# Channel-major partitions for the tiles of the first cross-attention of a gated two-layer block

## What is computed

```
x = x + tanh(g_xattn[0]) * L0_xattn(ctx, ctx, layernorm(x), ssm_kernel, D)
x = x + tanh(g_ffn[0])   * L0_ffn(layernorm(x), w1, b1, w2, b2)
x = x + tanh(g_xattn[1]) * L1_xattn(layernorm(x), ctx, ...)
x = x + tanh(g_ffn[1])   * L1_ffn(layernorm(x), ...)

L0_xattn: 32 heads of 8 channels; for channels i, j of one head
  kv[b,i,j,h,l] = ctx[b,i,h,l] * ctx[b,j,h,l]
  y = causal convolution of kv over l with ssm_kernel[h], plus D[h] * kv
  out[b,j,h,l] = sum over i of y[b,i,j,h,l] * q[b,i,h,l]
L0_ffn: int8 quantised linear 512 -> 2048, gelu, int8 quantised linear 2048 -> 512
```

## Time and profile before

| | |
|---|---|
| median of three runs | 734.99 us |
| the profiled execution's own time | 737.37 us |
| its span | 735.6 us |
| PE busy | 629.7 us (86%) |
| DVE busy | 547.1 us (74%) |
| ACT busy | 487.4 us (66%) |
| POOL busy | 345.8 us (47%) |
| bytes moved by DMA | 118.91 MB |

### The profile page before, as it was taken

How to read it: one execution, slowest core, us unless ns; L and a number is a source line. 1 busy time by engine, 2 the same in 40 slices (tenths; PEclk the granted TensorE clock), 3 DMA queues, 4 the chain that set the end, 5 groups by cost and what they waited for, 6 DMA issues and landing times.

```text
span 735.6 us, 9513 instructions
## 1 busy us (share of the span) xinstructions
PE 629.7 (86%) x2838; PEld 370.0 (50%) x2838; DVE 547.1 (74%) x1068; ACT 487.4 (66%) x726; POOL 345.8 (47%) x435
## 2 busy tenths in 40 slices
PE   3618619889999897992999999999989799999997
PEld 3416417667777663441454445555554344444443
DVE  2120636786899788781977799998998899999975
ACT  1302126757769656781997733776776999999985
POOL 1121445776878561750200001110336888989862
PEclk7667769999999998896999999999999999999999
DMA  3323466669999994123149199200012366656561
GB/s 107 116 105 119 140 198 222 221 206 318 343 282 330 403 300 160 54 103 138 57 126 357 44 171 249 66 14 14 15 29 57 116 172 173 190 169 198 155 188 43
DMA packets 127861, 118.91 MB, mean 162 GB/s; under 512 B 83456, under 2 KB 90384, under 8 KB 126672
## 3 DMA queue, kind: packets, MB, share of 16 engines
q1 hardware_dynamic: 120120, 103.71, 46.1%
q10 hardware_dynamic: 7704, 14.76, 6.3%
HBM read 68.04 MB, written 30.49 MB: 134 GB/s over the span
## 4 chain that ended last, share of the span: by engine, by line
PE 52%; DVE 14%; ACT 9%; SPq 8%; DMA 7%; issue 6%; POOL 2%; ACTq 0%; DVEq 0%; POOLq 0%
PE ps L1240 15%; PE ps L1502 12%; PE ps L1518 7%; PE ps L1330 4%; SPq L382 4%; ACT turn L1020 4%; PE ps L1429 3%; PE ps L1459 3%; SPq L391 2%; DMA arena<-in_x 2%; DMA x_d<-arena 2%; SPq L475 2%; PE ps L1477 2%; PE ps L1433 1%; DMA tern_d<-late 1%
## 5 line engine op out<-in xcount | busy, mean ns | idle before, releaser
L1240 PE MATMUL ps<-arena 128*128 128x288 f32 x640 | 174.7, 431 | 33.5 <-ACT arena L789 17.5
L1240 PEld LDWEIGHTS ps<-arena 128*128 128x128 f32 x640 | 127.0, 203 | 71.2 <-issue 20.2
L1502 PE MATMUL ps<-arena 128*128 128x512 bf16 x512 | 113.7, 379 | 4.3 <-DVE arena L2094 4.3
L629 POOL TENSOR_TENSOR arena<-arena 128x1024 f32<-128x1024 f32 x31 | 58.7, 1894 | 60.7 <-PE ps L1251 34.2
L733 POOL TENSOR_TENSOR arena<-arena 128x512 f32<-128x512 f32 x64 | 80.4, 1279 | 8.9 <-DVE arena L2094 8.1
L1502 PEld LDWEIGHTS ps<-arena 128*128 128x128 bf16 x512 | 49.6, 98 | 66.3 <-DVE arena L2094 3.6
L1330 PE MATMUL ps<-arena 128*128 128x512 bf16 (+1 forms) x256 | 61.2, 399 | 15.0 <-ACT arena L970 13.9
L1653 DVE TENSOR_TENSOR turn<-ps,arena 128x768 f32<-128x768 f32 x32 | 30.6, 955 | 43.4 <-PE ps L1251 43.3
L970 ACT ACTIVATE arena<-ps,b,s 128x512 f32<-128x512 f32 x64 | 46.1, 787 | 23.2 <-DMA x_d<-arena 15.3
L1518 PE MATMUL ps<-arena 128*128 128x512 bf16 x256 | 58.2, 379 | 1.0 <-ACT arena L1134 0.7
L1371 PE MATMUL ps<-arena 128*128 128x512 bf16 x256 | 55.6, 379 | 0.4 <-DVE arena L1843 0.4
(11 more groups left out here) (225 smaller groups left out, 1310.4 us busy)
## 6 DMA issues: line engine op xcount, KB each, us to landing
arena<-in_L_ffn_w SPq DMA_DIRECT2D x48, 512.0 KB, 6.4
arena<-kpad_d ACTq DMA_DIRECT2D x16, 512.0 KB, 6.0
hq_d<-arena SPq DMA_DIRECT2D x14, 512.0 KB, 2.6
tern_d<-late SPq DMA_DIRECT2D x24, 256.0 KB, 6.0
arena<-in_x SPq DMA_DIRECT2D x16, 256.0 KB
arena<-in_L_ffn_w ACTq DMA_DIRECT2D x8, 512.0 KB, 4.7
arena<-in_ctx SPq DMA_DIRECT2D x2, 2048.0 KB
x_d<-arena SPq DMA_DIRECT2D x16, 256.0 KB
```

The source lines that it names most:

```text
L629: pool.tensor_tensor(dst[:, :, 0:32].rearrange("p r (d i) -> p r d i", d=4), a, shifted, ALU.mult)
L1240: last = pe.matmul(ps[:, 4 * s + lo, 0:NB * PAIRS], toep[:, u, (LB - 1 - lo + li) * P:(LB - lo + li) * P], kv[:, s, li, :], start=(li == 0 ...
L1502: last = pe.matmul(ps[:, bank, :], xq4T[:, s, 4 * j + k, :], w[:, k, c * L:(c + 1) * L], start=(k == 0), stop=(k == LB - 1))
```

## The change

The partitions of a tile now hold 4 * channel + batch. All that touches this order follows:

- Loads and the stores to `x1_d` name 32 channels outermost and four batches inside, where they named four batches and then 32 channels. Bytes, the length of one contiguous piece (2 KB), number and order of the DMAs stay the same.
- `ctxT` and `qT` hold batch innermost. The eight channels of a head are then 16 bytes apart for each batch, so that `head_rows` yields single values 16 bytes apart instead of runs of eight. `repeat_c`, `repeat_q` and the last addition of a head go through it.
- `repeat_q` is written as two instructions of 256 values instead of one of 512, because of the number of dimensions.
- `rows_out` copies straight, without reordering. The rows of the quantised layer are thus in the order tile, channel, batch up to Gelu, whose output pattern restores batch, tile, channel: consecutive values are written 512 bytes apart.

```diff
-        ctxT = cut(32, ROWS * DM).rearrange("p (g r c) -> p g r c", g=2 * G, r=ROWS)
+        ctxT = cut(32, ROWS * DM).rearrange("p (g a c b) -> p g a c b", g=2 * G, a=2 * LB, b=G)
...
         def head_rows(m, h):
-            return m[:, h // G, :, HD * (h % G):HD * (h % G) + HD]
+            return m[:, h // G, :, HD * (h % G):HD * (h % G) + HD, :].rearrange("p a c b -> p a b c")
+
+        def by_batch(m):
+            return m.rearrange("p (a b) i -> p a b i", b=G)
...
-            return rows.rearrange("(s b) (g c) l -> s g b c l", b=G, c=CG)[n % 2, n // 2]
+            return rows.rearrange("(s b) (g c) l -> s g c b l", b=G, c=CG)[n % 2, n // 2]
...
-                        sp.dma_start(x1_d[at:at + CG, first:first + 2 * G - 1:2, :].rearrange("c b l -> b c l"),
+                        sp.dma_start(x1_d[at:at + CG, first:first + 2 * G - 1:2, :],
                                      tile_home(x_res[:, order1[n], :])).then_inc(S["x1_saved"], 16)
...
-                pool.tensor_tensor(head_rows(qT, h), x[:, :, 0:8], x[:, :, 8:16], ALU.add).then_inc(S["o_done"], 1)
+                pool.tensor_tensor(head_rows(qT, h), by_batch(x[:, :, 0:8]), by_batch(x[:, :, 8:16]), ALU.add).then_inc(S["o_done"], 1)
...
-                act.activation(cdup[:, u, :, 0:8], csr, ACT.Copy)
-                act.activation(cdup[:, u, :, 8:12], csr[:, :, 0:4], ACT.Copy).then_inc(S["cd_ready"], 1)
+                act.activation(by_batch(cdup[:, u, :, 0:8]), csr, ACT.Copy)
+                act.activation(by_batch(cdup[:, u, :, 8:12]), csr[:, :, :, 0:4], ACT.Copy).then_inc(S["cd_ready"], 1)
...
-                act.activation(qdup[:, u].rearrange("p r (d i) -> p r d i", d=2),
-                               head_rows(qT, h).unsqueeze(2).to_broadcast([P, ROWS, 2, 8]),
-                               ACT.Copy).then_inc(S["qd_ready"], 1)
+                for first in (0, 8):
+                    last = act.activation(by_batch(qdup[:, u, :, first:first + 8]), head_rows(qT, h), ACT.Copy)
+                last.then_inc(S["qd_ready"], 1)
...
-                    act.activation(hid[:, q, f, :], ps[:, f % 4, :],
+                    act.activation(hid[:, q, f, :].rearrange("p (b j c) -> p j c b", b=G, j=G),
+                                   ps[:, f % 4, :].rearrange("p (j c b) -> p j c b", b=G, j=G),
                                    ACT.Gelu, bias=b1[:, f:f + 1], scale=s1[:, f:f + 1]).then_inc(S["gelu_done"], 1)
...
-                    src = bank_bf(4 + 2 * (g % 2), 2).rearrange("p (j k b c) -> p j k b c", j=G, k=LB, b=G)
-                    dst = xqT[:, :, g * L:(g + 1) * L].rearrange("p k (b j c) -> p j k b c", b=G, j=G)
-                    last = v.tensor_copy(dst[:, tiles], src[:, tiles])
+                    last = v.tensor_copy(xqT[:, :, g * L:(g + 1) * L].rearrange("p k (j n) -> p j k n", j=G)[:, tiles],
+                                         bank_bf(4 + 2 * (g % 2), 2).rearrange("p (j k n) -> p j k n", j=G, k=LB)[:, tiles])
```

More of the change, by code:

```diff
@@ L89, in flamingo_gated_block @@
         x_res = cut(0, NT * L).rearrange("p (t l) -> p t l", t=NT)
-        ctxT = cut(32, ROWS * DM).rearrange("p (g r c) -> p g r c", g=2 * G, r=ROWS)
+        ctxT = cut(32, ROWS * DM).rearrange("p (g a c b) -> p g a c b", g=2 * G, a=2 * LB, b=G)
         xn1 = [cut(at, NT // 2 * L).rearrange("p (b l) -> p b l", b=NB) for at in (112, 48)]
-        qT = cut(64, ROWS * DM).rearrange("p (g r c) -> p g r c", g=2 * G, r=ROWS)
+        qT = cut(64, ROWS * DM).rearrange("p (g a c b) -> p g a c b", g=2 * G, a=2 * LB, b=G)
         ctx_raw = [turn[:, n * L:(n + 1) * L] for n in range(8)] + [cut(112 + 2 * n, L) for n in range(8)]
@@ L349, in channels @@
         def channels(m, n):
-            return m[:, n // 2].rearrange("p (l h b) c -> p l h (b c)", l=LB, h=2)[:, :, n % 2, :]
+            return m[:, n // 2].rearrange("p (l h) c b -> p l h (c b)", h=2)[:, :, n % 2, :]
         def back_rows(n, l):
-            at = l * NB + n % 2 * G
-            return qT[:, n // 2, at:at + G, :].rearrange("p b c -> p (b c)")
+            return qT[:, n // 2, 2 * l + n % 2].rearrange("p c b -> p (c b)")
         def head_rows(m, h):
-            return m[:, h // G, :, HD * (h % G):HD * (h % G) + HD]
+            return m[:, h // G, :, HD * (h % G):HD * (h % G) + HD, :].rearrange("p a c b -> p a b c")
+        def by_batch(m):
+            return m.rearrange("p (a b) i -> p a b i", b=G)
         def backwards(row):
@@ L1718, in _ @@
             dv.wait()
-            v.tensor_tensor(head_rows(qT, HEADS - 1), x[:, :, 0:8], x[:, :, 8:16], ALU.add).then_inc(S["o_done"], 1)
+            v.tensor_tensor(head_rows(qT, HEADS - 1), by_batch(x[:, :, 0:8]), by_batch(x[:, :, 8:16]), ALU.add).then_inc(S["o_done"], 1)
             slot_add(TAIL - 1)
```

## The result

| | before | after |
|---|---|---|
| median | 735.27 us (4 runs, 734.73 to 737.88) | 692.27 us (4 runs, 690.51 to 693.5) |
| ratio | 1 | 0.9407, 95% interval 0.9376 to 0.9437 |
| profiled execution, own time | 737.37 us | 693.5 us |
| its span | 735.6 us | 691.7 us |
| PE busy | 629.7 us | 625.3 us |

The change saves 43 us. The forecast was 689 us, and its own range 680 to 700.

What follows compares the result with a forecast made beforehand. PE was taken to bound, ACT second, after an opening held up by four-engine tile loads. Terms -52 - 17 + 18 + 5 = -46 on 737.4 us gave 691, forecast 689 us as a median; range 662 to 704, own range 680 to 700.

Steps and rivals of the forecast that it cites:

- The opening: Tile loads before head 5: 16 DMA engines in place of four move head 5 from 109.3 to 57.3 us, -52 us.
- The stores: Stores to scratch in the quantised layer: ACT's 15.3 us wait goes and PE's 2.1 us of slower pace, -17 us.
- Gelu: Quantised layer: writes 512 bytes apart lengthen each Gelu from 0.79 to 1.2 us, 26 us of ACT, +18 come through.
- cover: ACT's idle ahead of its Gelus beyond the removed stores' wait, taken to hide 8 us of Gelu's 26 us excess.
- rival (A): ACT's writes and reads of values apart cost nothing; sum -68, 667 us; chance 0.30.
- The copies of a head: ACT's `repeat_c` and `repeat_q` in the heads: reads 16 bytes apart cost up to 0.7 us a head, +5 us.
- three late heads and three heads waiting for an x tile: Heads where ACT's slower copies were to show: late ones also widening weights, and those awaiting an x tile (0.7 us each).
- POOL's write: POOL's L638 in a head: at 2.8 ns a value already slower than a write of single values, 0 added.
- `rows_out`: DVE's copy keeps its length, as it already ran in long runs; 0.
- Rival (B): The opening gains a third less than 52 us, through HBM hops or Toeplitz loads meeting tiles; 706 us; chance 0.11.
- rival (C): DMAs still run on four engines, so the waits stay and only +18 and +5 remain; 758 us; chance 0.03.
- Rival (D): ACT pays several steps for each value apart, Gelu at 2.0 us; slower, about 775 us; chance 0.04.

Runs made afterwards that it cites:

- gelu_straight: The changed kernel, but Gelu writes adjacent values and the transposes of the quantised rows use an identity with permuted columns; 675.52 us, ratio 0.9153 to the kernel before.
- reads_adjacent: `gelu_straight` with `head_rows` naming eight adjacent values, so a head's batches and channels are mixed; 672.51 us, ratio 0.9098 to the kernel before.
- loads_25_7: The changed kernel with each tile load split into a DMA of 25 channels and one of 7; 723.08 us, ratio 0.9798 to the kernel before.
- gelu_ctx_straight: `gelu_straight` with context tiles also transposed against a permuted identity, so `repeat_c` reads runs of eight; 672.35 us, ratio 0.9107 to the kernel before.

## Why the prediction was right

**The opening, -52 us: -50.7.** The path was as laid out: `kpad` stored at 8.9 us (forecast 8.5), head 0 at 16.97 (15), head 1 at 29.43 (28.5), head 3 at 41.77 (41), head 5 at 58.59 (57.3). Most of the gap of 1.3 us arose before head 0: a context tile, issued behind the stop of SP, was waited for until 15.21 us. That the rate follows the outermost count is shown from both sides: 101 GB/s at four, 387 at thirty-two, 148 with 25 and 7, each with what else moved in its window. That agrees with the rule of the Trainium skill that the prediction cited (DMA: Bandwidth & Descriptors, section "Why a DMA increments its semaphore by 16 and not by 1"), by which these would be 4, 16, and 5 and 7 engines.

**The stores, -17 us: -15.4**, from `gelu_straight` against before. No instruction of ACT waits for the stores any more. The term was the sum of the wait (15.3) and 2.1 us of PE's slower pace; but since PE waits 13.5 us and not 15.3, 13.5 + 2.1 = 15.6 was the right sum: I counted the wait on ACT and the slowdown on PE.

**Gelu, +18 us: +16.7.** Forecast 1.2 us a Gelu, measured 1.34. The mean overstates it, since neighbours overlap: over the stage ACT is busy 21.2 us more, 0.33 us a Gelu, where I had 0.41 and 26. Of the 8 us that I took as cover only 4.5 were: ACT still idles 3.5 us ahead of its Gelus, 1.62 of it for PE's first result, as in `gelu_straight`. So the sum was 21.2 - 4.5, not 26 - 8, and that the term came out within 1.3 us is luck in part: an excess 5 us too large beside a cover 3.5 us too large. PE's own pace doesn't set the stage, since PE waits 13.2 us for Gelu in it. That this term exists at all was the choice against rival (A), which would have been 667; the pair L1655 and L1657 carried it, and its 0.8 ns a value stands beside 0.9 measured in the mean of single Gelus.

**The copies of a head, +5 us: +5.8, in part for other reasons.** Single copies cost what I took (L810 at 653 ns, forecast 0.6 us). But the reads account for only 2.2 us, in two heads. 1.4 us is a wait further on, 4.15 us in place of 2.73:

```profile
206.59 7.45 PE L1243 MATMUL ps<-arena 128*128 128x288 f32 x20 [4.15 <-POOL arena L632]
```

It stays in `reads_adjacent` (4.19 us), so taking the strides away doesn't remove it. In all these kernels ACT waits for a weight DMA just ahead of the copies of this head, 5.21 us in the kernel before, 6.32 in `reads_adjacent`, and in the kernel after:

```profile
199.02 1.15 ACT L877 ACTIVATE late<-arena,inv_s 128x1024 int16<-128x1024 f32 x1 [3.81 <-DMA arena<-in_L_ffn_w]
```

The rest, 2.1 us, is PE at lower clock behind two idles (8.07 and 7.45 us for the 20 matmuls of a head, where before had 6.67 and 6.78); in `gelu_straight` they were 7.68 and 6.78, so this part differs from run to run. My three late heads and three heads waiting for an x tile were not what paid: the sum of 5 was right, its parts were not, and that is luck.

**POOL's write, 0: 0** (732 against 725 ns). `rows_out`, 0: nothing in the marks speaks against it.

The terms sum to -43.6 where -46 was forecast (the span moved by -43.9). Rival (B), the opening gaining a third less, and rival (C), still four engines, fell with the opening; `loads_25_7` shows what (B) would have looked like. Rival (D), several steps for each value, fell with Gelu at 1.34 us. Rival (A), that writing and reading apart is free, fell with the 16.7 us.

## What to carry to other kernels

Look at the DMA share while a stage only loads: a quarter of full was four engines here, and the outermost count of the access pattern in HBM decided it. Naming 32 channels there in place of four batches, at the same bytes and pieces, freed the opening. The price of the new layout then comes where single values are taken out of it: when ACT writes to SBUF keep at least two values within 16 bytes, by walking the pattern in another order with the jumps in PSUM, or by permuting the identity of a transpose that is there anyway. ACT, which was covered before, bounded a stage after 21 us of such cost; the same gain from loads can be had without it (672 against 692 us).

## What the runs showed of the hardware

- ACT's writes to SBUF have two prices, not a price per jump: 827 to 873 ns for 512 f32 with two or more values in 16 bytes, 1281 to 1333 ns with one, from 16 bytes apart to 512.
- ACT's reads from SBUF 16 bytes apart cost 0.97 ns a value (653 against 405 ns for 256), its reads from PSUM 16 bytes apart nothing (794 against 792 ns for 512).
- POOL's write of single values 16 bytes apart costs nothing that shows beside its 2.8 ns a value (732 against 725 ns for 256).
- With tile loads of 25 + 7 channels all DMAs together moved 148 GB/s, with loads of 32 channels 387 in the window from 20 to 28.5 us, with 16 + 16 252. In the last SP took 0.63 us to issue one DMA of 0.131 MB, which by itself allows 207 GB/s of tiles (an estimate); head 5 came no later by it than 0.2 us (58.79 against 58.59).
- A transpose on PE against an identity with permuted columns takes as long as one against the plain identity: 16 in bf16 take 1.86 us in `gelu_straight` and in the kernel after, 8 in f32 1.04 us in `gelu_ctx_straight` and in the kernel after.
